# Weight splits moved behind the first graph's own steps, and more idle transposes on PE

## Chip, cores and metric

One core of a Trainium2 chip. The metric is the device time of the whole kernel in microseconds (us), median of several runs.

## What is computed

32 graphs of 256 nodes with 256 features go through four blocks, each with a residual and a layer norm. Cut to what matters here, for one graph (`x`, `adj`, all 256 x 256):

```
agg = adj @ x / deg(adj);   x1 = LN(x + relu([x, agg] @ W0^T))
h = relu(adj @ (x1 @ W1) + b1);  h = relu(adj @ (h @ W2) + b2)
x2 = LN(x1 + adj @ (h @ W3) + b3)
q, k, v = x2 @ W_qkv                      # 8 heads of 64
p = 0.33 * (softmax(q k^T / 8) + adj + exp(-adj))
x3 = LN(x2 + (p v) @ W_out + b_out)
q, k, v = x3 @ W3_qk^T, x3 @ W_v^T;  w = softmax(sum(q k^T * adj) / 8)
x4 = LN(x3 + w * v)
```

The graphs are independent of each other; the weights are shared.

## The kernel before

Matrix products run in fp32r with operands split in two: a high part (`_h`, a copy with rounding) and a low part (`_l`, the rest), and three products (hh, hl, lh) are summed. ACT makes every high part (`copy`, all recorded at L320), DVE every low part (`lo`, L555). PE's products are at L922 (`product`), 12 matmuls for one 256 x 256 x 256 product of nodes; they are called in two parts: HI (8 matmuls, needs only the high part of the operand that comes late) and LO (4 matmuls, needs the low part). Transposes of data are at L936, `keep_busy` is at L943: it transposes the identity into a bank that nobody reads, so many times.

Each engine has a hand-written list of steps, `slot(s)`, that runs for s = -2 to 35. Graph g's early steps stand in the lists of slot g - 1 and g, its attention and tail in slots g to g + 3, so that in the middle of the run each engine works on several graphs in turn. An engine executes its list strictly in order: a step that waits holds up all behind it. Only graph 0 runs nearly alone at the start. Its chain is: support0 (x @ W0's second half), sup0 split, aggregate (adj @ sup0), x1's norm (DVE, POOL, DVE), x1 transposes, then three layers of support (@ W1, W2, W3) and hidden / gcn_out (adj @ ...), x2's norm, x2 transposes, then the products with W_qkv.

The weights come by DMA and are split once, when g == 0. A count `act_w` tells how many high parts are done, `dve_w` how many low parts: w0 is 1; W1, W2, W3 are 2, 3, 4; the two halves of W_qkv (k = 0, 1) are 5, 6; W_out is 7; the last block's weight (w3) is 8. PE waits for these numbers in `weights(g, number)`. In the kernel before, the splits are attached to these steps of graph 0:

- ACT: w0 behind `x_hi`; W1, W2, W3 behind `sup0_hi`, and so ahead of `adj_hi`; both halves of W_qkv behind `x1_hi`; W_out and w3 behind `sup_hi(0)`.
- DVE: w0 behind `x_lo`; W1 behind `sup0_lo`, ahead of `adj_lo`; W2, W3 behind `norm_mean(0)`; W_qkv's halves behind `x1_lo` and `sup_lo(0)`; W_out and w3 behind `hidden_lo(0)`.

The order of ACT around it: x_hi(0), degrees(0), sup0_hi(0), adj_hi(0), adj_exp(0), self_copy(0), x1_hi(0), sup_hi(0), x_hi(1), hidden(0), hidden_hi(0), sup_hi(1), hidden(1), hidden_hi(1), sup_hi(2), x2_hi. That of DVE: x_lo(0), degrees(0), sup0_lo, adj_lo, aggregate, relu_residual, norm 0, x1_lo, sup_lo(0), adj_sum, hidden_lo(0), x_lo(1), sup_lo(1), x1_bias, hidden_lo(1), adj_extra, sup_lo(2), gcn_out, norm 1, x2_lo. `keep_busy` stands ahead of the mask columns (5), ahead of the loop (18), in front of the x1 transposes (40) and the x2 transposes (30) of graph 0, and in front of the last x3 transposes (30).

Of the kernel before, what the change touches and what calls it, by code (L numbers as in the profile page):

```python
# [13 lines left out]
def graph_blocks_kernel(nc, x, adj, nodemask, xT, adjT_in, L0_WT, L1_W1, L1_b1, L1_W2, L1_b2, L1_W3, L1_b3,  # L14
# [4 lines left out]
    FT = F // P  # L19
    D = 64  # L20
# [15 lines left out]
    with ctx:  # L36
        def sb(name, shape, dt=F32):
            return ctx.enter_context(nc.sbuf_tensor(name, shape, dt))
# [9 lines left out]
        w123_raw = sb("w123_raw", [P, 3, FT, F])  # L48
        work = sb("work", [P, 2, 2 * NT * 2 * N])
        wqkv_raw = work[:, :, 0:3 * INNER]  # L50
        wout_raw = sb("wout_raw", [P, PAIRS, F])
        w3_raw = sb("w3_raw", [P, FT, L3C])
# [11 lines left out]
        w123 = [sb(f"w123_{s}", [P, 3, FT, F], F32R) for s in "hl"]  # L64
        wqkv = [sb(f"wqkv_{s}", [P, FT, 3, INNER], F32R) for s in "hl"]
        wout = [sb(f"wout_{s}", [P, PAIRS, F], F32R) for s in "hl"]
        w3 = [sb(f"w3_{s}", [P, FT, L3C], F32R) for s in "hl"]
# [95 lines left out]
        def halves(ap):  # L163
            return ap.rearrange("p (a b) -> p a b", a=2)
# [37 lines left out]
        def once(g):  # L202
            return min(g + 1, G)
# [7 lines left out]
        def live(g):  # L211
            return 0 <= g < G

        def loaded(g):
            return 16 * (g // 2 + 1)

        def reuse(eng, semaphore, n):

            if n > 0:
                eng.wait_ge(semaphore, n)  # L220


        W0, W1, W2, W3TH, W_QKV, W_OUT, W_LAST = 1, 2, 3, 4, 5, 7, 8
# [94 lines left out]
        def _(act):  # L318
            def copy(dst, src, scale=1.0):
                return nc.scalar.activation(dst, src, ACT.Copy, scale=scale)  # L320

            def weight_hi(dst, src):
                return copy(dst, src).then_inc(act_w, 1)
# [18 lines left out]
            def adj_hi(g):  # L342
                if not live(g):
                    return
                act.wait_ge(dma_adjT[g % 2], loaded(g))
                reuse(act, pe_adjk, once(g - 2))
                copy(adjT[0][:, g % 2], adjT_sb[:, g % 2]).then_inc(act_adjT, 1)

            def degrees(g):
                if not live(g):  # L350
# [25 lines left out]
            def sup0_hi(g):  # L376
                if not live(g):
                    return
                act.wait_ge(pe_sup0, once(g))
                copy(sup[0][:, :, :], halves(bank(SUP0))).then_inc(act_sup0, 1)  # L380
                if g == 0:
                    act.wait_ge(dma_w123, 16 * 3)
                    for i in range(3):
                        weight_hi(w123[0][:, i], w123_raw[:, i])

            def self_copy(g):
                if not live(g):
# [4 lines left out]
            def x1_hi(g):  # L392
                if not live(g):
                    return
                act.wait_ge(pe_x1T, once(g))
                copy(fT[0][:, :, :], halves(bank(X1T))).then_inc(act_x1T, 1)
                if g == 0:
                    act.wait_ge(dma_wqkv, 16)
                    for k in range(FT):
                        weight_hi(wqkv[0][:, k].rearrange("p i (h d) -> p i h d", d=D),  # L400
                                  wqkv_raw[:, k].rearrange("p (h i d) -> p i h d", i=3, d=D))

            def sup_hi(layer, g):
                if not live(g):
                    return
                act.wait_ge(pe_sup[layer], once(g))
                copy(sup[0][:, :, :], halves(bank(SUP[layer]))).then_inc(act_sup[layer], 1)
                if g == 0 and layer == 0:
                    act.wait_ge(dma_wout, 16)
                    weight_hi(wout[0][:, :, :], wout_raw[:, :, :])  # L410
                    act.wait_ge(dma_w3, 16)
                    weight_hi(w3[0][:, :, :], w3_raw[:, :, :])
# [135 lines left out]
        def _(dve):  # L548
# [5 lines left out]
            def lo(dst, src, hi_part):  # L554
                return V_.tensor_tensor(dst, src, f32(hi_part), ALU.subtract)  # L555

            def weight_lo(dst, src, hi_part, number, last=True):
                dve.wait_ge(act_w, number)
                step = lo(dst, src, hi_part)
                if last:  # L560
                    step.then_inc(dve_w, 1)

            def wqkv_lo(k):
                for i in range(3):
                    weight_lo(wqkv[1][:, k, i].rearrange("p (h d) -> p h d", d=D),
                              wqkv_raw[:, k].rearrange("p (h i d) -> p i h d", i=3, d=D)[:, i],
                              wqkv[0][:, k, i].rearrange("p (h d) -> p h d", d=D), W_QKV + k, last=i == 2)
# [52 lines left out]
            def adj_lo(g):  # L620
                if not live(g):
                    return
                dve.wait_ge(act_adjT, once(g))
                reuse(dve, pe_adjk, once(g - 2))
                lo(adjT[1][:, g % 2], adjT_sb[:, g % 2], adjT[0][:, g % 2]).then_inc(dve_adjT, 1)

            def degrees(g):
                if not live(g):
# [25 lines left out]
            def sup0_lo(g):  # L654
                if not live(g):
                    return
                dve.wait_ge(act_sup0, once(g))
                lo(sup[1][:, :, :], halves(bank(SUP0)), sup[0][:, :, :]).then_inc(dve_sup0, 1)
                if g == 0:
                    weight_lo(w123[1][:, 0], w123_raw[:, 0], w123[0][:, 0], W1)  # L660

            def aggregate(g):
                if not live(g):
# [32 lines left out]
            def x1_lo(g):  # L696
                if not live(g):
                    return
                dve.wait_ge(act_x1T, once(g))
                lo(fT[1][:, :, :], halves(bank(X1T)), fT[0][:, :, :]).then_inc(dve_x1T, 1)  # L700
                if g == 0:
                    wqkv_lo(0)

            def sup_lo(layer, g):
                if not live(g):
                    return
                dve.wait_ge(act_sup[layer], once(g))
                lo(sup[1][:, :, :], halves(bank(SUP[layer])), sup[0][:, :, :]).then_inc(dve_sup[layer], 1)
                if g == 0 and layer == 0:
                    wqkv_lo(1)  # L710

            def hidden_lo(layer, g):
                if not live(g):
                    return
                dve.wait_ge(act_hid_hi[layer], once(g))
                lo(hidT[1][:, :, :], hid[:, :, :], hidT[0][:, :, :]).then_inc(dve_hid[layer], 1)
                if g == 0 and layer == 0:
                    weight_lo(wout[1][:, :, :], wout_raw[:, :, :], wout[0][:, :, :], W_OUT)
                    weight_lo(w3[1][:, :, :], w3_raw[:, :, :], w3[0][:, :, :], W_LAST)

            def gcn_out(g):
                if not live(g):
# [186 lines left out]
        def _(pe):  # L909
# [30 lines left out]
            def keep_busy(free_bank, count):  # L940

                for _ in range(count):
                    nc.tensor.transpose(bank(free_bank)[:, 0:P], ident[:, :], ident[:, :])  # L943
# [9 lines left out]
            def weights(g, number):  # L953
                if g == 0:
                    pe.wait_ge(dve_w, number)
# [41 lines left out]
            def x1_transpose(g):  # L997
                if not live(g):
                    return
                if g == 0:  # L1000
                    keep_busy(7, 40)
                pe.wait_ge(dve_x[0], once(g))
                transpose_tiles(bank(X1T), x1).then_inc(pe_x1T, 1)

            def support(layer, g, part):
                if not live(g):
                    return
                if part == HI:
                    weights(g, W1 + layer)
                    if layer == 0:  # L1010
                        pe.wait_ge(act_x1T, once(g))
                        reuse(pe, dve_scores, nth2(g - 1, 2, 1))
                    if layer == 1:
                        pe.wait_ge(act_hid_hi[0], once(g))
                    if layer == 2:
                        pe.wait_ge(act_hid_hi[1], once(g))
                else:
                    if layer == 0:
                        pe.wait_ge(dve_x1T, once(g))
                    if layer == 1:  # L1020
                        pe.wait_ge(dve_hid[0], once(g))
                    if layer == 2:
                        pe.wait_ge(dve_hid[1], once(g))
                last = nodes_product(bank(SUP[layer]), hidT if layer else fT, [w[:, layer] for w in w123], part)
                if part == LO:
                    last.then_inc(pe_sup[layer], 1)
# [228 lines left out]
            pe.wait_ge(pool_ident, 2)  # L1255
            keep_busy(7, 5)
            mask_columns()
            keep_busy(7, 18)
            for s in range(FIRST, LAST):
                slot(s)  # L1260

# [27 lines left out]
```

## Time and profile before

| | us |
|---|---|
| median of 3 runs | 1386.93 (1386.03 to 1387.05) |
| the profiled execution | 1388.81 |
| its span | 1387.0 |
| PE busy (matmuls) | 1358.5 (98%) |
| DVE busy | 1227.9 (89%) |
| ACT busy | 912.3 (66%) |
| POOL busy | 124.5 (9%) |

The span is from the first to the last instruction of one profiled execution. The profile has, for each engine, groups of instructions in order of time, the idle time ahead of a group and who ended it, and for stretches of time the busy time and PE's granted clock as a share of 2.4 GHz (0.50 is 1.2 GHz). PE is busy nearly throughout; the first 50 us and the last 50 us have gaps.

### The profile page before, as it was taken

How to read it: one execution, taken by the hardware profiler on the slowest of the kernel's cores; microseconds unless marked ns; L12 is line 12 of the kernel's file. 1: busy time of each engine (PE TensorE's matmuls, PEld its weight loads, DVE VectorE, ACT ScalarE, POOL GpSimd, SP SyncE). 2: the span in 40 equal slices, each digit the busy share in tenths (PEclk: the TensorE clock that was granted, in tenths of full speed). 3: DMA queues.
4: the chain of work that ended last, by engine and by line, in shares of the span. 5: the costliest groups of instructions: out<-in, count | busy, mean ns of one | idle time of the engine just before them, and what ended most of it. 6: DMA issues, size and time to landing. Idle time of an engine off the chain costs nothing.

```text
span 1387.0 us, 30079 instructions
## 1 busy us (share of the span) xinstructions
PE 1358.5 (98%) x11005; PEld 1196.8 (86%) x11005; DVE 1227.9 (89%) x3820; ACT 912.3 (66%) x2444; POOL 124.5 (9%) x265
## 2 busy tenths in 40 slices
PE   6999999999999999999999999999999999999996
PEld 6888889888889888889888889888889888889884
DVE  5689999999999999999999999999999999999985
ACT  4466776666776666776666777666776666776663
POOL 0000101101001101101101101101101101101101
PEclk9899999999999999999999999999999999999998
DMA  5111001111011111001111011111001111001000
GB/s 180 33 32 32 11 30 40 40 41 40 11 31 40 40 40 41 12 30 40 41 40 40 10 32 40 40 41 40 13 29 40 40 40 41 14 28 40 9 9 23
DMA packets 51313, 48.99 MB, mean 35 GB/s; under 512 B 7904, under 2 KB 50656, under 8 KB 51168
## 3 DMA queue, kind: packets, MB, share of 16 engines
q1 hardware_dynamic: 51168, 47.08, 10.7%
q8 instruction: 88, 1.44, 0.4%
q14 instruction: 57, 0.47, 0.1%
HBM read 38.68 MB, written 8.39 MB: 34 GB/s over the span
## 4 chain that ended last, share of the span: by engine, by line
PE 95%; ACT 2%; DVE 1%; issue 0%; DMA 0%; SPq 0%; POOL 0%; POOLq 0%; DVEq 0%
PE psum L922 63%; PE psum L936 12%; PE psum L1127 9%; PE psum L1104 8%; PE psum L1179 1%; PE psum L1182 1%; PE psum L1192 1%; PE psum L1201 0%; DMA w_raw<-in_L_gnn_W 0%; PE psum L943 0%; ACT work L454 0%; DVE work L767 0%; ACT wqkv_h L320 0%; ACT w_h L320 0%; DVE bn L571 0%
## 5 line engine op out<-in xcount | busy, mean ns | idle before, releaser
L454 ACT ACTIVATE work<-work,shift 128x256 f32<-128x256 f32 x512 | 253.9, 500 | 44.9 <-DVE shift L748 44.9
L767 DVE SCALAR_TENSOR_TENSOR work<-work,rsum,extra 128x256 f32<-128x256 f32 x512 | 221.2, 479 | 1.2
L748 DVE CUSTOM_DVE_ANT_0 work<-psum,minus_big 128x256 f32<-128x256 f32 x512 | 192.7, 419 | 16.5 <-PE psum L1104 15.4
L320 ACT ACTIVATE work<-psum 128x512 f32<-128x512 f32 x256 | 144.5, 594 | 9.7 <-PE psum L936 9.7
L922 PE MATMUL psum<-x2T_h,wqkv_h 128*128 128x256 f32 x512 | 148.7, 290 | 1.3 <-DVE x2T_l L555 1.2
L922 PE MATMUL psum<-x2T_l,wqkv_h 128*128 128x256 f32 x512 | 142.2, 278 | 0.0
L922 PE MATMUL psum<-x2T_h,wqkv_l 128*128 128x256 f32 x512 | 142.1, 278 | 0.0
L936 PE MATMUL psum<-ident,work 128*128 128x128 f32 x1024 | 139.7, 274 | 0.7 <-DVE work L767 0.7
L302 POOL TENSOR_TENSOR mv<-mv,eps 128x2 f32<-128x2 f32 x128 | 25.6, 200 | 1248.4 <-DVE mv L592 1248.4
L1127 PE MATMUL psum<-work,v_sb 128*64 128x256 f32 x1024 | 131.9, 389 | 0.9 <-ACT work L320 0.9
L320 ACT ACTIVATE sup_h<-psum 128x512 fp32r<-128x512 f32 x128 | 76.4, 597 | 74.0 <-PE psum L922 74.0
L555 DVE TENSOR_TENSOR sup_l<-psum,sup_h 128x512 fp32r<-128x512 f32 x128 | 88.1, 688 | 37.4 <-ACT sup_h L320 37.4
L936 PEld LDWEIGHTS psum<-ident,work 128*128 128x128 f32 x1024 | 113.5, 140 | 6.1 <-DVE work L767 1.3
L320 ACT ACTIVATE qkT_h<-psum 128x512 fp32r<-128x512 f32 x128 | 75.8, 592 | 39.0 <-PE psum L922 39.0
L922 PEld LDWEIGHTS psum<-x2T_h,wqkv_h 128*128 128x128 f32 x512 | 96.1, 188 | 6.1 <-DVE x2T_l L555 1.5
L922 PE MATMUL psum<-w_h,fT_h 128*128 128x256 f32 x384 | 100.1, 296 | 1.2 <-ACT fT_h L320 0.8
L305 POOL TENSOR_TENSOR rstd<-mv,minus_half 128x2 f32<-128x2 f32 x128 | 99.2, 775 | 10.0
L1127 PEld LDWEIGHTS psum<-work,v_sb 128*64 128x64 f32 x1024 | 64.9, 136 | 40.1 <-issue 6.9
L454 ACT ACTIVATION_READ_ACCUMULATOR work<-work,shift 128x1 f32 x512 | 97.8, 191 | 0.0
L571 DVE BATCH_NORM_STATS2 bn<-x_pre 128x6 f32<-128x256 f32 x256 | 95.8, 416 | 1.2
L922 PEld LDWEIGHTS psum<-x2T_l,wqkv_h 128*128 128x128 f32 x512 | 96.2, 188 | 0.0
L922 PEld LDWEIGHTS psum<-x2T_h,wqkv_l 128*128 128x128 f32 x512 | 96.1, 188 | 0.0
(130 smaller groups left out, 3806.2 us busy)
## 6 DMA issues: line engine op xcount, KB each, us to landing
xT_sb<-in_xT SPq DMA_DIRECT2D x32, 256.0 KB, 2.8
adjT_sb<-in_adjT SPq DMA_DIRECT2D x32, 256.0 KB, 3.1
adj_sb<-in_adj SPq DMA_DIRECT2D x32, 256.0 KB, 4.2
x_sb<-in_x SPq DMA_DIRECT2D x32, 256.0 KB, 4.4
out<-y_sb SPq DMA_DIRECT2D x32, 256.0 KB, 2.2
work<-in_L_gnn_W_qkv SPq DMA_DIRECT2D x1, 1536.0 KB, 9.8
mask_row<-in_nodemask SPq DMA_DIRECT2D x32, 32.0 KB, 4.1
w_raw<-in_L_gnn_W SPq DMA_DIRECT2D x3, 256.0 KB, 5.4
```

What stands on the lines that cost most here:

```text
L302: nc.gpsimd.tensor_tensor(mv[:, k, :, 1], mv[:, k, :, 1], eps[:, :], ALU.add) \
L305: nc.gpsimd.tensor_tensor(rstd[:, k], mv[:, k, :, 1], minus_half[:, :], ALU.pow) \
L320: return nc.scalar.activation(dst, src, ACT.Copy, scale=scale)
L454: last = nc.scalar.activation(prob[:, p % 2, i, h], prob[:, p % 2, i, h], ACT.Exp, bias=shift[:, p % 2, h, i:i + 1], scale=-1.0, accum_out ...
L555: return V_.tensor_tensor(dst, src, f32(hi_part), ALU.subtract)
L571: last = V_.bn_stats(out=bn[:, k, t], in_=src[:, t])
L748: last = V_.tensor_tensor_reduce(out=prob[:, p % 2, i, h], in0=bank(SCORES[p] + h)[:, i * N:(i + 1) * N], in1=minus_big[:, g % 2, i], scal ...
L767: last = V_.scalar_tensor_tensor(out=prob[:, p % 2, i, h], in0=prob[:, p % 2, i, h], scalar=rsum[:, p % 2, h, i:i + 1], in1=extra[:, g % 2 ...
L922: last = mm(dst, left, right, start=opens and n == 0, stop=closes and n == len(steps) - 1)
L936: last = nc.tensor.transpose(dst[:, r * N + t * P:r * N + (t + 1) * P], src[:, t, block_of(r)], ident[:, :])
L1104: last = mm(bank(SCORES[p] + h)[:, i * N:(i + 1) * N], qkT[left][rows, p % 2, 0, block_of(i)], qkT[right][rows, p % 2, 1], start=n == 0 an ...
L1127: last = mm(bank(PV[p])[h * D:(h + 1) * D, 0:N], v_sb[:, k, (2 * p + h) * D:(2 * p + h + 1) * D], probT[:, p % 2, h, k], start=k == 0, sto ...
```

## The change

All edits are for graph 0 or ahead of the loop:

- ACT: W1, W2, W3 are copied behind `adj_hi` instead of `sup0_hi`; the W_qkv halves one by one behind `sup_hi(0)` and `sup_hi(1)` instead of both behind `x1_hi`; W_out and w3 behind `sup_hi(2)` instead of `sup_hi(0)`.
- DVE: W1's low part behind `adj_lo` instead of `sup0_lo`; the W_qkv halves behind `sup_lo(0)` and `sup_lo(1)` instead of `x1_lo` and `sup_lo(0)`; W_out and w3 behind `sup_lo(2)` instead of `hidden_lo(0)`.
- PE: `keep_busy` 40 to 44 in front of the x1 transposes; 12 new ones in front of support 1 and of support 2, each; 18 to 21 ahead of the loop.

No transfer, semaphore or count is changed. The functions `degrees` to `sup0_hi` of ACT, which the printed diff moves, are the same text.

```diff
             def adj_hi(g):
                 copy(adjT[0][:, g % 2], adjT_sb[:, g % 2]).then_inc(act_adjT, 1)
+                if g == 0:
+                    act.wait_ge(dma_w123, 16 * 3)
+                    for i in range(3):
+                        weight_hi(w123[0][:, i], w123_raw[:, i])
...
             def sup0_hi(g):
                 copy(sup[0][:, :, :], halves(bank(SUP0))).then_inc(act_sup0, 1)
-                if g == 0:
-                    act.wait_ge(dma_w123, 16 * 3)
-                    for i in range(3):
-                        weight_hi(w123[0][:, i], w123_raw[:, i])
...
             def x1_hi(g):
-                if g == 0:
-                    act.wait_ge(dma_wqkv, 16)
-                    for k in range(FT):
-                        weight_hi(wqkv[0][:, k].rearrange("p i (h d) -> p i h d", d=D),
-                                  wqkv_raw[:, k].rearrange("p (h i d) -> p i h d", i=3, d=D))
...
             def sup_hi(layer, g):
-                if g == 0 and layer == 0:
+                if g == 0 and layer < 2:
+                    act.wait_ge(dma_wqkv, 16)
+                    weight_hi(wqkv[0][:, layer].rearrange("p i (h d) -> p i h d", d=D),
+                              wqkv_raw[:, layer].rearrange("p (h i d) -> p i h d", i=3, d=D))
+                if g == 0 and layer == 2:
                     act.wait_ge(dma_wout, 16)
                     weight_hi(wout[0][:, :, :], wout_raw[:, :, :])
                     act.wait_ge(dma_w3, 16)
...
             def adj_lo(g):
+                if g == 0:
+                    weight_lo(w123[1][:, 0], w123_raw[:, 0], w123[0][:, 0], W1)
...
             def sup0_lo(g):
-                if g == 0:
-                    weight_lo(w123[1][:, 0], w123_raw[:, 0], w123[0][:, 0], W1)
...
             def x1_lo(g):
-                if g == 0:
-                    wqkv_lo(0)
...
             def sup_lo(layer, g):
-                if g == 0 and layer == 0:
-                    wqkv_lo(1)
+                if g == 0 and layer < 2:
+                    wqkv_lo(layer)
+                if g == 0 and layer == 2:
+                    weight_lo(wout[1][:, :, :], wout_raw[:, :, :], wout[0][:, :, :], W_OUT)
+                    weight_lo(w3[1][:, :, :], w3_raw[:, :, :], w3[0][:, :, :], W_LAST)
...
             def hidden_lo(layer, g):
-                if g == 0 and layer == 0:
-                    weight_lo(wout[1][:, :, :], wout_raw[:, :, :], wout[0][:, :, :], W_OUT)
-                    weight_lo(w3[1][:, :, :], w3_raw[:, :, :], w3[0][:, :, :], W_LAST)
...
             def x1_transpose(g):
                 if g == 0:
-                    keep_busy(7, 40)
+                    keep_busy(7, 44)
...
             def support(layer, g, part):
                 if part == HI:
+                    if g == 0 and layer:
+                        keep_busy(7, 12)
                     weights(g, W1 + layer)
...
             keep_busy(7, 5)
             mask_columns()
-            keep_busy(7, 18)
+            keep_busy(7, 21)
```

## Rows read from the trace of the kernel before

**Rows 1.** The page: the span.

```profile
span 1387.0 us, 30079 instructions
```

**Rows 2.** Windows, stretch, length, busy PE, PEld, DVE, ACT, POOL, clock, DMA.

```profile
60.00:1340.00 1280.00, 1278.55 (x10445) 1127.19 (x10444) 1164.98 (x3637) 864.93 (x2330) 117.46 (x244) 1.00 0.10 32
```

**Rows 3.** Timeline of ACT: start, us, what, [idle before <-releaser]; around adjT.

```profile
11.20 1.67 ACT L320 ACTIVATE w_h<-w_raw 128x512 fp32r<-128x512 f32 x3 [1.04 <-DMA w_raw<-in_L_gnn_W]
12.77 0.61 ACT L320 ACTIVATE adjT_h<-adjT_sb 128x512 fp32r<-128x512 f32 x1
...
13.81 0.57 ACT L320 ACTIVATE self_part<-psum 128x512 f32<-128x512 f32 x1
```

**Rows 4.** Timeline of ACT, from x1's transposes to the first hidden layer.

```profile
23.33 2.85 ACT L320 ACTIVATE wqkv_h<-work 128x1536 fp32r<-128x1536 f32 x2
...
26.55 1.06 ACT L320 ACTIVATE wout_h<-wout_raw 128x1024 fp32r<-128x1024 f32 x1
...
28.75 0.84 ACT L421 ACTIVATE hid<-psum,b_col 128x256 f32<-128x256 f32 x2
29.62 0.63 ACT L320 ACTIVATE hidT_h<-hid 128x512 fp32r<-128x512 f32 x1
```

**Rows 5.** Timeline of DVE, first graph.

```profile
10.19 0.69 DVE L555 TENSOR_TENSOR sup_l<-psum,sup_h 128x512 fp32r<-128x512 f32 x1 [1.66 <-ACT sup_h L320]
...
16.81 0.88 DVE L668 SCALAR_TENSOR_TENSOR x_pre<-psum,rdeg,self_part 128x256 f32<-128x256 f32 x2 [2.70 <-PE psum L922]
...
24.84 1.90 DVE L555 TENSOR_TENSOR wqkv_l<-work,wqkv_h 128x512 fp32r<-128x512 f32 x3 [0.69 <-ACT wqkv_h L320]
...
30.89 1.22 DVE L555 TENSOR_TENSOR wout_l<-wout_raw,wout_h 128x1024 fp32r<-128x1024 f32 x1
32.03 0.95 DVE L555 TENSOR_TENSOR w_l<-w_raw,w_h 128x768 fp32r<-128x768 f32 x1
...
43.99 0.69 DVE L725 TENSOR_TENSOR x_pre<-psum,x_b 128x512 f32<-128x512 f32 x1 [2.29 <-PE psum L922]
...
46.84 0.74 DVE L608 TENSOR_SCALAR x<-x_pre,mv,rstd 128x256 f32<-128x256 f32 x2 [1.08 <-POOL rstd L305]
```

**Rows 6.** Timeline of PE, first graph: first row of each burst, transposes.

```profile
14.21 0.35 PE L922 MATMUL psum<-sup_h,adjT_h 128*128 128x256 f32 x1 [3.28 <-ACT adjT_h L320]
...
16.48 5.34 PE L943 MATMUL psum<-ident 128*128 128x128 f32 x40
22.14 0.66 PE L936 MATMUL psum<-ident,x 128*128 128x128 f32 x4 [0.31 <-DVE x L608]
...
26.72 0.39 PE L922 MATMUL psum<-adjT_h,sup_h 128*128 128x256 f32 x1 [1.53 <-ACT sup_h L320]
...
30.40 0.36 PE L922 MATMUL psum<-w_h,hidT_h 128*128 128x256 f32 x1 [1.98 <-ACT hidT_h L320]
...
32.84 0.58 PE L922 MATMUL psum<-adjT_h,sup_h 128*128 128x256 f32 x1 [0.69 <-ACT sup_h L320]
...
37.44 0.55 PE L922 MATMUL psum<-w_h,hidT_h 128*128 128x256 f32 x1 [1.68 <-ACT hidT_h L320]
...
47.86 0.60 PE L936 MATMUL psum<-ident,x 128*128 128x128 f32 x4
...
49.97 0.36 PE L922 MATMUL psum<-x2T_h,wqkv_h 128*128 128x256 f32 x1
```

**Rows 7.** Windows, PE alone: stretch, length, busy (matmuls), granted clock, DMA.

```profile
1.60:7.40 5.80, 5.76 (x25) 1.00 0.87 277
14.80:18.00 3.20, 3.20 (x18) 0.50 0.90 356
18.20:21.80 3.60, 3.60 (x33) 1.00 0.92 342
25.20:31.60 6.40, 2.90 (x22) 1.00 0.00 0
31.80:45.40 13.60, 10.54 (x47) 0.50 0.00 0
```

## The prediction

> **What bounds the kernel now.** I read the page first, for the span [rows 1], then the busy time of each engine in one long stretch, then the beginning engine by engine. From 60 to 1340 us PE is busy 1278.55 of 1280 us [rows 2]. DVE has 1164.98 and ACT 864.93 in the same stretch. The reader is to see that all 32 graphs after the start are one gapless queue on PE: the time is the moment at which PE becomes gapless, plus a fixed queue, plus a tail. The change leaves queue and tail as they are (every edited line stands under `g == 0` or ahead of the loop), so an earlier start of the gapless stretch is worth its whole length, and an earlier ACT or DVE alone is worth nothing. That stretch begins with the first query and key product at 49.97 [rows 6]. I follow that product back.
>
> PE's rows of the first graph show short bursts, each waiting for ACT: 3.28 us before the aggregation, then 1.53, 1.98, 0.69 and 1.68 us [rows 6]. The bursts cost by the granted clock. The one from 30.40 takes 1.75 us (32.84 less its 0.69 idle), the one from 32.84 takes 2.92 (37.44 less 1.68), for the same 12 matmuls. The clock is at 2.4 GHz (1.00) from 18.2 and at 1.2 GHz (0.50) from 31.8 to 45.4 [rows 7]. So the change can gain in two ways: shorter waits, and bursts at the higher level.
>
> **Part 1, adj_hi ahead of the three W1..W3 copies.** Before, ACT waits for the DMA of the last of them until 11.20, spends 1.67 us on three copies, and only then copies adjT (12.77); DVE's adj_lo follows and PE's aggregation starts at 14.21 [rows 3, 6]. After, adj_hi stands behind sup0_hi. DVE's sup_l starts at 10.19 [rows 5], so sup_h is finished by then and ACT starts adjT_h there: done at about 10.8, the lo part of 0.69 us at 11.5, PE at about 11.6. The burst costs 1.7 us if the clock holds (2.3 at the old level), so it ends at 13.3. The three copies still start at 11.20, as their DMA sets them. What was 12.77 (adjT_h, 0.61) isn't between them and self_part any more, so self_part moves from 13.81 to 13.29 and ends at 13.86 [rows 3]. DVE's aggregate step needs both; it is self_part now that comes last, and the step starts at 13.93 instead of 16.81 [rows 5]: **2.88 us**. W1's lo part, moved behind adj_lo, runs before that in DVE's wait and costs nothing. Three more idle transposes ahead of the loop cost 3 x 0.23 = 0.7 us (25 took 5.8, [rows 7]). If none of it lies in PE's wait for w0, the burst ends at 14.0, 0.1 past self_part; if all of it does, nothing is late. I take nothing.
>
> **Part 2, wqkv's halves out of x1_hi and x1_lo.** From DVE's aggregate step to the end of support 0 nothing else changes: the x1 transposes come 5.33 us after the step (22.14 - 16.81), at 19.26, and support 0 ends 3.05 us behind them (25.19, which is 26.72 less 1.53, minus 22.14) [rows 5, 6], at 22.31. Then ACT's sup_hi was held up by the two wqkv copies, 2.85 us from 23.33 [rows 4]; the wait of PE was 1.53, where the undisturbed one of the next layer is 0.69. After, it is 0.68, so hidden 0 starts at 22.99: another **0.85 us**, 3.73 in sum against 26.72. It takes 1.70 (28.42 - 26.72) and ends at 24.69. One wqkv copy (half of 2.85, with x_hi of 0.5 behind it) now lies between: 22.9 to 24.8, so hidden's ReLU starts at 24.8 instead of 24.72, nearly free. ReLU and hidT_h take 0.84 and 0.63 [rows 4]; support 1 starts at 26.39. Before 30.40: **4.0 us**.
>
> **Part 3, the clock from there.** DVE does wqkv_lo(0) from 24.36 (1.90 us, [rows 5]), then adj_sum (0.6), so hidden_lo starts at 26.8, some 0.5 late; support 1's last four matmuls wait until 27.55, and it ends at 28.25, 0.1 later than without. The first half of wqkv being enough for none of PE's work, nobody else waits. hidden 1: 28.25 + 0.69 = 28.93, ends 30.63 at the higher level. ACT has wqkv(1) from 28.8 to 30.2, inside that burst: free. ReLU and copy, 1.67 with gaps (37.44 - 35.76): support 2 starts at 32.30. DVE: wqkv_lo(1) to 32.1, x1_bias to 32.7, hidden_lo until 33.4, so the last part of support 2 starts at 33.5 and it ends at 34.15, 0.1 to 0.3 late. gcn_out starts at 34.83 and ends at 36.53. Before, gcn_out's sum in DVE started at 43.99 [rows 5].
>
> **Part 4, what is late next: wout and w3.** They now stand behind sup_lo(2), in front of DVE's gcn_out step. ACT copies wout 34.7 to 35.75 (1.06, [rows 4]), DVE's lo parts follow at 35.82 for 1.22 and 0.95 (0.08 less back to back) [rows 5] and end at 37.83. The gcn_out step is ready at 36.55 and so waits **1.3 us** behind them, and all that hangs on it: bn, POOL, x2, x2T. Step at 37.83 instead of 43.99: 6.16 earlier. From it to x2 ready takes 3.59 (46.84 + 0.74 - 43.99, [rows 5]): 41.42. Before, PE's 30 idle transposes still stood in front of x2's own, by 0.2 us (47.86 against 47.63, [rows 6]). After they end near 39.5, and x2's start at 41.47; the first query product follows 2.11 behind (49.97 - 47.86), with support 0 of the next graph in between as before: 43.6. That is **49.97 - 43.6 = 6.4 us** less.
>
> **The transposes in the waits** (12 and 12 new, 40 made 44) are 0.11 us each at 2.4 GHz (33 in 3.6 us) and up to 0.23 at 1.2 [rows 7]: 12 are 1.3 us in waits of 1.7, free; at 1.2 GHz they would be 2.6 to 2.8 and outlast the wait by about 1.0. The 44 run from 13.3 to 18.2, and leave 1.0 us idle before 19.26.
>
> The Trainium skill, "TensorE: Matmul & The Clock Gate", Part 4, states that transpose mode doesn't count as PE being busy for the gate. By that rule these transposes would be useless or worse, and the time (c)'s, below. The trace speaks against it: the clock was at 0.50 from 14.8 to 18.0, the transposes began at 16.48, and at 18.2 to 21.8, with 33 of them and nothing else on PE, it was 1.00 [rows 6, 7].
>
> Does the gain add up to the end? The loads of graph 2 are released by the first graph's steps and shift with them. The profiled execution took 1388.81 us for a span of 1387.0, 1.9 above the median of the runs, 1386.93. I take the difference of spans from the median: 1386.93 - 6.35 = 1380.6.
>
> **Rivals.**
> (a) The clock falls once. Before, it fell after 25.2 to 31.6, where PE was busy 2.90 of 6.40 us [rows 7]. The forecast has two thin stretches: 18.2 to 23.0 (idle 1.0, 0.8, 0.7 between short bursts) and 39.5 to 42 (idle 1.9). Neither is quite like the stretch that lost the clock, and neither is as full as those that kept it; the trace doesn't settle it. If it falls near 21.5, hidden 0 costs 2.92 for 1.70 (1.2) and 12 transposes outlast their wait (up to 1.6 more, less once the clock is back; PE is then busy without a gap): 1.2 to 2.8, I take 2.0. If it falls at 42, PE is busy from there, and before, it was low in such a busy stretch for at least the 3.2 us from 14.8 to 18.0 [rows 7], at half speed: 1.6 to 1.7 lost. So 1382.3 to 1382.6 us.
> (b) It falls in both: 1380.6 + 3.7 = 1384.3.
> (c) Slower than before: idle transposes don't hold the clock, and at the low level they are in the way. Decides if PE stays at 0.50 from the x1 wait on. Then hidden 0, support 1, hidden 1, support 2 and gcn_out cost 1.2 more each (6.0), support 0's rest 0.5, the two twelves 1.0 each, less 1.3 since wout's parts are hidden again: gcn_out's sum at 37.83 + 7.2 = 45.0, and the 30 transposes behind it at 0.23 (6.9) end at 51.8 against 47.9 before, so +3.9: 1390.8. Its condition is what the page states; the windows of 14.8 to 21.8 [rows 7] speak against it.
> (d) The splits don't hold DVE or ACT up as I say: wout and w3 cost gcn_out nothing: 1.3 us more gain, 1379.3. Or the first stretch is set by other DMAs than now, and only the clock and 0.85 us are gained: some 3.5, 1383.4.
>
> **How the numbers follow.** Forecast 1380.6: chance 0.43. (a) 0.32, (b) 0.12, (c) 0.04, (d) 0.04 for its first, 0.05 for its second. Range 1379.4 to 1384.4: it leaves out (c), (d)'s first and up to half of (b), 0.14 in all. The forecast's own range is 1380.0 to 1381.4. 0.2% of this kernel, 2.8 us, is about what a measurement can tell: faster means below 1384.2. Forecast, (a), (d) and half of (b) lie there: 0.43 + 0.32 + 0.09 + 0.06 = 0.90; within 0.2% the rest of (b), 0.06; slower (c), 0.04.
>
> **What would show it.** DVE's aggregate step at 13.9 with self_part just before it (part 1). PE's wait before hidden 0 at 0.7 (part 2). Granted clock 1.00 from 18 to 40, and bursts of 1.7 us (part 3). wout_l and w_l right in front of gcn_out's sum, PE long done (part 4). First query product at 43.6, then the same gapless queue. A clock of 0.50 anywhere between 20 and 46 is (a) or (b). The prediction is wrong if PE's gapless stretch begins 6 us earlier and the end doesn't move with it.

## The result and the profile after

| | before | changed |
|---|---|---|
| median of 10 runs | 1386.80 us (1384.73 to 1387.54) | 1383.65 us (1382.49 to 1384.66) |
| ratio, changed to before | | 0.9977, 95% interval 0.9968 to 0.9986 |
| the profiled execution | 1388.81, span 1387.0 | 1384.66, span 1382.9 |

The change gains 3.15 us by the medians and 4.1 us from one profiled span to the other. The measured 1383.65 us lies within the range, and the direction is right. But the forecast was 1380.6 us, and half of the gain it named (6.2) isn't there in the median.

The middle is what it was. PE's window of the changed kernel (stretch, length, busy, granted clock, DMA):

```profile
60.00:1340.00 1280.00, 1278.52 (x10444) 1.00 0.10 32
```

The first query product, the row of PE's timeline that answers to the last of [rows 6]:

```profile
45.90 0.36 PE L919 MATMUL psum<-x2T_h,wqkv_h 128*128 128x256 f32 x1
```

PE is as gapless as in [rows 2], and the gapless stretch begins at 45.90 instead of 49.97: 4.07 us earlier, for a span 4.1 us shorter. From that product to the end both profiles take 1337.0 us, so all of the gain comes from the first 46 us. (One gap of 0.43 to 0.44 us, 4.5 us behind the product, is in both.) ACT's timeline in the changed kernel, which answers to [rows 3]:

```profile
9.80 0.63 ACT L320 ACTIVATE adjT_h<-adjT_sb 128x512 fp32r<-128x512 f32 x1
11.51 1.68 ACT L320 ACTIVATE w_h<-w_raw 128x512 fp32r<-128x512 f32 x3 [1.08 <-DMA w_raw<-in_L_gnn_W]
...
13.61 0.57 ACT L320 ACTIVATE self_part<-psum 128x512 f32<-128x512 f32 x1
```

DVE's, which answers to [rows 5]:

```profile
14.21 0.88 DVE L667 SCALAR_TENSOR_TENSOR x_pre<-psum,rdeg,self_part 128x256 f32<-128x256 f32 x2 [1.35 <-ACT self_part L320]
...
38.10 1.22 DVE L554 TENSOR_TENSOR wout_l<-wout_raw,wout_h 128x1024 fp32r<-128x1024 f32 x1 [0.26 <-ACT wout_h L320]
39.24 0.95 DVE L554 TENSOR_TENSOR w_l<-w_raw,w_h 128x768 fp32r<-128x768 f32 x1
40.11 0.68 DVE L722 TENSOR_TENSOR x_pre<-psum,x_b 128x512 f32<-128x512 f32 x1
```

adjT is copied ahead of the three weights, and DVE's aggregate step starts at 14.21 instead of 16.81, now released by self_part. The low parts of W_out and w3 stand without a gap in front of gcn_out's sum at 40.11 (43.99 before). Timeline of PE, which answers to [rows 6]:

```profile
12.83 4.97 PE L940 MATMUL psum<-ident 128*128 128x128 f32 x44
19.54 0.66 PE L933 MATMUL psum<-ident,x 128*128 128x128 f32 x4 [1.74 <-DVE x L607]
...
24.26 0.58 PE L919 MATMUL psum<-adjT_h,sup_h 128*128 128x256 f32 x1 [0.69 <-ACT sup_h L320]
...
26.98 2.05 PE L940 MATMUL psum<-ident 128*128 128x128 f32 x12
...
38.71 3.44 PE L940 MATMUL psum<-ident 128*128 128x128 f32 x30
43.74 0.66 PE L933 MATMUL psum<-ident,x 128*128 128x128 f32 x4 [1.59 <-DVE x L607]
```

PE's windows in the same kernel, in the columns of [rows 7]:

```profile
12.80:17.80 5.00, 5.00 (x46) 1.00 1.05 387
17.80:21.00 3.20, 0.69 (x5) 1.00 1.03 375
21.50:28.00 6.50, 5.81 (x27) 0.50 0.05 18
28.50:50.00 21.50, 17.98 (x147) 1.00 0.14 40
```

After 5 us without a gap PE has 0.69 us of work in 3.20, and then the clock is at 0.50, from before 21.5 until past 28.0. Most of support 0 (from 20.97) and all of hidden 0 (from 24.26) run in that stretch at 1.2 GHz. That is rival (a) in its first form.

### The profile page after: what moved, and what is told of

It reads as the page before. It is cut to its first block, busy times and chain, and to the rows that moved or that the text cites. A ratio compares the mean times of both kernels' runs of the same rounds, so it can differ in the third digit from the quotient of the medians.

```text
span 1382.9 us, 30141 instructions
## 1 busy us (share of the span) xinstructions
PE 1358.4 (98%) x11036; PEld 1197.1 (87%) x11036; DVE 1227.9 (89%) x3820; ACT 912.5 (66%) x2444; POOL 124.4 (9%) x265
## 4 chain that ended last, share of the span: by engine, by line
PE 95%; DVE 2%; ACT 1%; DMA 0%; issue 0%; SPq 0%; POOL 0%; POOLq 0%; DVEq 0%
PE psum L919 63%; PE psum L933 12%; PE psum L1126 9%; PE psum L1103 8%; PE psum L1178 1%; PE psum L1181 1%; PE psum L1191 1%; PE psum L1200 0%; DMA w_raw<-in_L_gnn_W 0%; ACT work L453 0%; DVE work L764 0%; DVE bn L570 0%; POOL rstd L305 0%; DVE x L607 0%; DVE wqkv_l L554 0%
```

## The experiments

Each kernel is the changed one with the edit shown, unless it says otherwise. The runs come from three sets, each on one chip and with the kernel before beside it. The row "changed" without a set is the result above, whose kernel before had 1386.80 us. Medians of different sets aren't strictly comparable: the time from the first query product to the end is 1336.9 to 1337.3 us in the ten profiles of before, the result and the first two sets, and 1338.1 to 1338.2 in the four of the third. No edit reaches there, and the changed kernel itself has 1337.0 in the result and 1338.1 in the third set, so times of the third set are some 1.2 us longer for that alone. "The twelves" are the 12 idle transposes in front of support 1 and of support 2. The ratios to before are those on record with the runs and aren't exactly the quotients of the medians.

Each run also gives its mean granted clock over the span. It is the number to group by, since it says how long an execution was at 1.2 GHz: 0.001 is 2.8 us of it. Part of that is the tail, where PE has little left to do.

```
kernel                        set  median   range               mean granted clock of the runs
before                        1    1387.28  1385.87 to 1391.18  0.988 to 0.995
before                        2    1387.03  1384.03 to 1391.53  0.986 to 0.996
before                        3    1387.71  1386.52 to 1392.37  0.990 to 0.996
changed                       -    1383.65  1382.49 to 1384.66  0.994 x4, 0.995 x2, 0.996 x4
x1 wait 58                    1    1383.24  1382.42 to 1384.51  0.996 x2, 0.997 x3
moves only                    1    1386.16  1382.19 to 1388.96  0.988 to 0.997
transposes only               1    1386.66  1385.49 to 1387.30  0.994 x7, 0.995 x1, 0.996 x3
low parts late                1    1381.45  1380.85 to 1382.90  0.996 x2, 0.997 x3
x1 wait 0                     2    1385.56  1383.62 to 1386.14  0.991 x2, 0.992 x7, 0.994 x2
part 1 undone                 2    1385.36  1383.95 to 1386.79  0.994 x4, 0.995 x4, 0.996 x3, 0.997 x1
part 2 undone                 2    1384.06  1383.09 to 1385.63  0.994 x3, 0.995 x1, 0.996 x6, 0.997 x1
part 1 alone                  2    1383.95  1382.62 to 1385.46  0.993 to 0.997
changed again                 3    1385.58  1383.62 to 1386.65  0.994 x1, 0.995 x4, 0.996 x3, 0.997 x3
58, no twelves                3    1383.85  1383.39 to 1386.97  0.992 x2, 0.995 x1, 0.996 x2, 0.997 x6
58 and low parts late         3    1382.78  1382.40 to 1383.41  0.997 x5
the same, W_qkv's lo later    3    1383.43  1382.88 to 1384.54  0.996 x1, 0.997 x4
```

**58 idle transposes in the x1 wait.** Does the idle stretch ahead of 21 us lose the clock?

```diff
-                    keep_busy(7, 44)
+                    keep_busy(7, 58)
```

> The changed kernel with 58 idle transposes instead of 44 in PE's wait for x1. Theory (the clock falls near 21 us because PE sits idle for 1.7 us there): 14 more at 0.11 us fill 1.5 of the 1.7 us, PE's granted clock stays at 1.00 from 8 us to the tail in every run, the first query product starts near 44.0 instead of 45.9, median 1382.5 against 1383.65 and no run above 1383. Rival (idle transposes don't count for the clock, or the 3.15 us gained are all there is): still 0.50 from 21 to 28, median 1383.7.

Measured 1383.24, ratio to before 0.9963 (0.9949 to 0.9977). PE's windows in its profile:

```profile
13.00:19.60 6.60, 6.60 (x63) 1.00 0.98 354
20.00:50.00 30.00, 24.20 (x198) 1.00 0.21 63
```

The start of x2's transposes in its timeline:

```profile
41.55 0.66 PE L933 MATMUL psum<-ident,x 128*128 128x128 f32 x4 [1.58 <-DVE x L607]
```

The mechanism is as expected: the clock at 1.00 from 13 us to the tail, no run below 0.996 where the changed kernel has six of ten, x2's transposes at 41.55 instead of 43.74, and a span of 1380.6. The median moved by 0.4 us and not by the 1.2 I expected. The two medians come from different sets (against its own set's before this kernel gains 4.04 us, the changed one 3.15), and three of the five runs are above 1383 (one at 1384.51), which I had ruled out. The 58 also outlast the wait a little: x1's transposes start 5.46 us behind DVE's aggregate step here and 5.33 in the changed kernel.

**No idle transposes in the x1 wait.**

```diff
-                    keep_busy(7, 44)
+                    keep_busy(7, 0)
```

> The changed kernel with no idle transposes in PE's wait for x1 (44 to 0), so that PE is idle there for some 6.6 us. Theory (idle transposes hold the clock): PE's granted clock falls to 0.50 in this wait in every run, and comes back only at the 12 transposes or later: 3 to 7 us more at the low level than the changed kernel's quickest runs, quickest run 1384 or above (1382.5 with 44), median 1385 to 1386. Rival (transposes don't count as work for the clock): the same as with 44, quickest 1382.5, median 1383.7.

Measured 1385.56, ratio 0.9988 (0.9979 to 0.9997); the quickest run is 1383.62, where I had 1384 or above, and every run is at 0.994 or below. PE's timeline at x1's transposes:

```profile
19.90 1.12 PE L933 MATMUL psum<-ident,x 128*128 128x128 f32 x4 [6.55 <-DVE x L607]
```

Its windows:

```profile
16.00:28.80 12.80, 7.43 (x32) 0.50 0.47 175
30.00:50.00 20.00, 16.53 (x131) 1.00 0.10 27
```

Idle for 6.55 us, PE is at 1.2 GHz from 16.0 to 28.8. The same wait filled with 58 transposes and nothing else keeps 2.4 GHz (13.0 to 19.6, above). Idle transposes do hold the clock here, and that is worth about 2 us of median (1.9 against the 44 and 2.3 against the 58, which are from other sets). By the Trainium skill, "TensorE: Matmul & The Clock Gate", Part 4, transpose mode doesn't count as PE being busy: by that, the two kernels would behave alike. The measurement decides against it for these fp32 transposes.

**The moves without the new transposes.** The splits as moved; 18, 40 and no twelves, as before.

```diff
-                    if g == 0 and layer:
-                        keep_busy(7, 12)
...
-                    keep_busy(7, 44)
+                    keep_busy(7, 40)
...
-            keep_busy(7, 21)
+            keep_busy(7, 18)
```

> The moved splits alone; idle transposes as before (18 ahead of the loop, 40 before x1, none before support 1 and 2). Theory (shorter waits give 4 us only if the clock holds, and the transposes hold it): the clock falls near 21 and stays at 0.50 until gcn_out or later, since nothing fills the waits of the hidden layers; five bursts at 2.9 instead of 1.7 us: 1382.5 + 6 - 1.3 = about 1387, no gain over before. Rival (the moves are the gain, the transposes are decoration): 1383.5 to 1384.

Measured 1386.16, ratio 0.9984 (0.9972 to 0.9997). Neither theory had this: the runs lie 6.8 us apart, in the order of their clock almost without exception. Two at 0.997 took 1382.19 and 1382.65, as quick as the changed kernel ever is; the two at 0.990 and 0.988 took 1388.66 and 1388.96. The profiled one is of the quick kind. A window of PE, and the start of x2's transposes:

```profile
20.00:50.00 30.00, 21.57 (x174) 1.00 0.21 65
```

```profile
41.60 0.66 PE L933 MATMUL psum<-ident,x 128*128 128x128 f32 x4 [1.59 <-DVE x L607]
```

The clock held though PE idles 1.97 us in front of x1's transposes and 1.75 and 1.68 us where the twelve are missing. So the same program on the same chip keeps the clock or loses it, from one execution to the next. What the moves shorten doesn't need the transposes, but having it in the median does.

**The transposes without the moves.** The kernel before, with 21, 44, 12 and 12.

```diff
-                    keep_busy(7, 40)
+                    keep_busy(7, 44)
...
+                    if g == 0 and layer:
+                        keep_busy(7, 12)
```

> The kernel before with the new idle transposes alone (21, 44, 12, 12), splits where they were. Theory: the clock that before loses from 31.8 to 45.4 us holds or comes back early, four bursts at 1.7 instead of 2.9 us: 3 to 5 us gained, median 1382 to 1384, all of it from the clock. Rival (the moves are the gain): 1386.8.

Measured 1386.66, ratio 0.999 (0.9982 to 0.9999). My theory missed: 0.6 us and not 3 to 5. PE's windows in its profile:

```profile
8.00:13.50 5.50, 2.78 (x24) 1.00 0.83 265
14.00:20.50 6.50, 5.36 (x25) 0.50 1.02 373
21.00:50.00 29.00, 23.43 (x189) 1.00 0.05 12
```

The start of the aggregation in its timeline:

```profile
15.14 0.55 PE L922 MATMUL psum<-sup_h,adjT_h 128*128 128x256 f32 x1 [4.36 <-ACT adjT_h L320]
```

The hidden layers do keep the clock now (21 to 50 at 1.00), which the profile of before didn't. The stretch in front of the aggregation, 4.36 us idle, still loses it, and the waits are as long as ever. Two things explain the small gain: the profiled execution of before, from which I took the 3 to 5 us, had lost more of the clock than most do, and the transposes can't save what part 1 saves.

**Low parts of W_out and w3 late.**

```diff
-                if g == 0 and layer == 2:
-                    weight_lo(wout[1][:, :, :], wout_raw[:, :, :], wout[0][:, :, :], W_OUT)
-                    weight_lo(w3[1][:, :, :], w3_raw[:, :, :], w3[0][:, :, :], W_LAST)
...
             def x2_lo(g):
+                if g == 0:
+                    weight_lo(wout[1][:, :, :], wout_raw[:, :, :], wout[0][:, :, :], W_OUT)
                 dve.wait_ge(act_x2T, once(g))
                 lo(x2T[1][:, :, :], halves(bank(X2T)), x2T[0][:, :, :]).then_inc(dve_x2T, 1)
+                if g == 0:
+                    weight_lo(w3[1][:, :, :], w3_raw[:, :, :], w3[0][:, :, :], W_LAST)
```

> The changed kernel with the low part of W_out in front of x2_lo and that of w3 behind it, instead of both in front of DVE's gcn_out. Theory (gcn_out's sum waits 1.4 us for them and is on the path): the sum starts when PE ends, near 38.8 instead of 40.1, PE's wait behind the 30 transposes falls from 1.6 to 0.2 us, and the median is 1.3 lower, 1382.3. Rival (hidden under the 30 idle transposes of PE, which end at 42.1): 1383.65.

Measured 1381.45, ratio 0.9952 (0.9936 to 0.9967): the quickest kernel of the study against its own runs of before. DVE's timeline in its profile:

```profile
36.62 0.69 DVE L719 TENSOR_TENSOR x_pre<-psum,x_b 128x512 f32<-128x512 f32 x1 [1.07 <-PE psum L920]
...
40.11 1.22 DVE L554 TENSOR_TENSOR wout_l<-wout_raw,wout_h 128x1024 fp32r<-128x1024 f32 x1
41.58 0.69 DVE L554 TENSOR_TENSOR x2T_l<-psum,x2T_h 128x512 fp32r<-128x512 f32 x1 [0.25 <-ACT x2T_h L320]
```

PE's:

```profile
40.25 0.66 PE L934 MATMUL psum<-ident,x 128*128 128x128 f32 x4 [0.40 <-DVE x L607]
```

The sum starts with PE's end, at 36.62. In the profile of the kernel with 58, whose clock is equally held, it starts at 37.92, and x2's transposes at 41.55 against 40.25: 1.30 us in both. Of these, 0.10 were there before: gcn_out's product starts at 34.98 with 58 and at 34.88 here. The wait itself is worth 1.2 us, and PE's idle time behind the 30 transposes falls by as much, from 1.59 to 0.40. The low part of W_out now ends 0.25 us before x2T_l is wanted. The median is 2.2 us below the changed kernel's (1.8 below that with 58, on the same chip), more than the 1.3 I expected. Part of the 2.2 is that none of these five runs is below 0.996, with the same 44 transposes in front of x1, which this edit doesn't touch; the rest isn't explained.

**Part 1 undone.** The three copies and W1's low part back behind sup0_hi and sup0_lo.

```diff
                 copy(adjT[0][:, g % 2], adjT_sb[:, g % 2]).then_inc(act_adjT, 1)
-                if g == 0:
-                    act.wait_ge(dma_w123, 16 * 3)
...
                 copy(sup[0][:, :, :], halves(bank(SUP0))).then_inc(act_sup0, 1)
+                if g == 0:
+                    act.wait_ge(dma_w123, 16 * 3)
```

> The changed kernel with part 1 undone: W1, W2, W3 split behind sup0_hi and sup0_lo again, ahead of adj_hi and adj_lo. Theory (part 1 is worth 2.6 to 2.9 us of waits, and is the bulk): DVE's aggregate step back near 16.8 instead of 14.2, quickest run 1385.2 against 1382.5; with the clock lost ahead of the aggregation as before, median 1386.3 or above. Rival (the gain is mostly the clock's, and the wait is refilled later): within 1 us of the changed kernel, 1384 to 1384.5.

Measured 1385.36, ratio 0.999 (0.9982 to 0.9999). The aggregate step in DVE's timeline:

```profile
18.24 0.88 DVE L667 SCALAR_TENSOR_TENSOR x_pre<-psum,rdeg,self_part 128x256 f32<-128x256 f32 x2 [3.13 <-PE psum L919]
```

It is past the 16.8 of before, since the weights' DMA landed late in this execution too and the clock was lost ahead of the aggregation. Against its own set's before, this kernel gains 1.67 us and the changed one 3.15, so part 1 carries about half of the gain. I had expected less to be left: a median above 1386.3 and a quickest run of 1385.2, which was 1383.95. By the runs at 0.996 (1385.17 here, 1382.88 in the changed kernel) part 1 is worth 2.3 us, by the medians 1.5 to 1.7. The profiles show where the rest of its 2.9 us goes. Here the clock is lost ahead of the aggregation (0.50 from 14 to 20 us) and is back for the hidden layers: from the copies of W1 to W3 to the aggregate step it takes 6.04 us (5.61 in before, 2.70 in the changed kernel), and from that step to x2's transposes 27.67. The changed kernel loses the clock behind the step and needs 29.53 for the same way, 27.59 with 58.

**Part 2 undone.** Both W_qkv halves back behind x1_hi, in DVE behind x1_lo and sup_lo(0).

```diff
                 copy(fT[0][:, :, :], halves(bank(X1T))).then_inc(act_x1T, 1)
+                if g == 0:
+                    act.wait_ge(dma_wqkv, 16)
+                    for k in range(FT):
...
-                if g == 0 and layer < 2:
-                    wqkv_lo(layer)
+                if g == 0 and layer == 0:
+                    wqkv_lo(1)
```

> The changed kernel with part 2 undone: both halves of W_qkv split behind x1_hi, and in DVE behind x1_lo and sup_lo(0), again. Theory: PE's wait before hidden 0 back at 1.5 us instead of 0.7 (0.85 more), of which 0.3 to 0.4 comes back since DVE has no W_qkv step ahead of x1_bias and hidden_lo(1): 0.4 to 0.8 slower by the quickest runs, median 1384.2. Rival (nothing waited for it in the end): 1383.65.

Measured 1384.06, ratio 0.9976 (0.9966 to 0.9987). PE's timeline before hidden 0, and before x2's transposes:

```profile
24.39 0.39 PE L922 MATMUL psum<-adjT_h,sup_h 128*128 128x256 f32 x1 [1.80 <-ACT sup_h L320]
...
42.43 0.66 PE L936 MATMUL psum<-ident,x 128*128 128x128 f32 x4 [1.59 <-DVE x L608]
```

From x1's transposes (19.55) to these of x2 it takes 22.88 us; with 58 and part 2 in, 22.13 (41.55 - 19.42), both with the clock held. Part 2 is worth 0.75 us on the path, of which ACT's wait for the DMA of W_qkv in this execution is 0.16. The medians put it at 0.4, and the gains against each one's own before at 0.2, both inside their uncertainty.

**Part 1 alone, with the new transposes.** Both halves of W_qkv as above, W_out and w3 back behind sup_hi(0) and hidden_lo(0). (What the expectation calls part 3 is part 4 of the prediction.)

```diff
-                if g == 0 and layer == 2:
+                if g == 0 and layer == 0:
                     act.wait_ge(dma_wout, 16)
```

> Parts 2 and 3 undone: only the W1 to W3 splits moved, and all the new idle transposes. Theory (part 3 moved 1.3 us of wait in front of gcn_out's sum, which eats what part 2 gained): W_out and w3 split early again, gcn_out's sum starts when PE ends; 0.85 lost before hidden 0 and 1.3 to 1.4 gained before x2: by the quickest runs 0.3 to 0.6 faster than the changed kernel, 1382.0, median 1383.2. Rival (parts 2 and 3 are a gain): 1384.3 to 1385.

Measured 1383.95, ratio 0.9982 (0.9974 to 0.9991). Neither side: not the 0.3 to 0.6 us quicker of my theory (quickest 1382.62, expected 1382.0), nor the rival's 1384.3. Two rows of its timeline say why, the first of ACT:

```profile
21.80 2.86 ACT L320 ACTIVATE wqkv_h<-work 128x1536 fp32r<-128x1536 f32 x2 [1.25 <-DMA work<-in_L_gnn_W_qkv]
```

and one of DVE:

```profile
40.22 0.69 DVE L725 TENSOR_TENSOR x_pre<-psum,x_b 128x512 f32<-128x512 f32 x1 [1.06 <-PE psum L922]
```

The second is as I had it: gcn_out's sum no longer waits for low parts. The first is new. With part 1 in, ACT is at W_qkv nearly 3 us sooner than before, ahead of its DMA, and waits 1.25 us for it. The copy of x1's support stands behind, and PE waits for it before hidden 0:

```profile
25.20 0.58 PE L922 MATMUL psum<-adjT_h,sup_h 128*128 128x256 f32 x1 [2.12 <-ACT sup_h L320]
```

In the kernel before, that DMA had landed 2.2 us before ACT came to it (issued at 11.3, 9.8 us to landing, copies from 23.33). So part 2 also takes a DMA wait off the path that part 1 had uncovered, 0.16 us in the profile with only part 2 undone and 1.25 here.

**The changed kernel again**, beside the next three.

> The changed kernel itself, beside the three others of this set on one chip. Expected median 1383.3 to 1384.0, quickest run near 1382.5, runs with 0 to 7 us of low clock at the start.

Measured 1385.58 (ratio 0.9978, 0.9969 to 0.9987), above the median I had expected. The recorded ratio is the one first measured, but by the medians the gain is 2.13 us here and was 3.15. The interval of each ratio reaches 1.2 us to either side, so the two gains don't contradict each other, and neither is known to better than about a microsecond. One row of ACT in its profile:

```profile
12.21 1.67 ACT L320 ACTIVATE w_h<-w_raw 128x512 fp32r<-128x512 f32 x3 [1.08 <-DMA w_raw<-in_L_gnn_W]
```

The last of W1 to W3 was there at 12.2; the other profiles have 11.20 to 12.20. self_part, and with it x1, follow it one to one (DVE's aggregate step at 14.92 here, 2.71 behind the copies; at 13.96 with 58, where they start at 11.25). It is the second thing that differs between executions, beside the clock, which this one lost too (x1's transposes at 20.24 behind an idle 1.72 us, the clock at 0.50 from 22.7 to 29.1).

**58, but no twelves.**

```diff
-                    if g == 0 and layer:
-                        keep_busy(7, 12)
...
-                    keep_busy(7, 44)
+                    keep_busy(7, 58)
```

> 58 idle transposes before x1, none before support 1 and 2. Theory (each wait needs its own filling, since the clock is decided again and again): some runs lose the clock in the hidden layers, where each loses 3 us or more for want of a gapless stretch: quickest 1382.4, median 1384 to 1385.5, slowest above 1387. Rival (the x1 wait alone decides, the two twelves are idle decoration): all runs 1382.4 to 1384, as with 58 and both twelves.

Measured 1383.85, ratio 0.9973 (0.9964 to 0.9982). Nine of the eleven runs are at 0.995 or above, within 1.3 us of each other; two lost the clock, at 1386.2 and 1387.0. The profiled one is one of them; PE's windows:

```profile
20.00:28.00 8.00, 4.74 (x34) 1.00 0.25 86
29.00:42.00 13.00, 9.95 (x44) 0.50 0.00 1
43.00:50.00 7.00, 6.91 (x59) 1.00 0.24 77
```

This is the stretch of 0.50 that the profile of before shows [rows 7]: once lost among the hidden layers' bursts it stays lost for 13 us, until the idle transposes before x2. The twelves are an insurance, rarely needed once x1's wait is full. The theory's mechanism holds; its median (1384 and more) was too high and its quickest run (1382.4, measured 1383.39) too low.

**58 and the low parts late.** The edits of the first and fifth experiment together.

> 58 idle transposes before x1, and W_out's and w3's low parts behind gcn_out's sum. Theory (two independent terms: clock 0.4 to 1.0 by the median, wait 1.3): median 1381.1, spread under 2 us, faster than each alone (1383.24 and 1381.45). Rival (not additive, since with the shorter x2 wait the clock is safe anyway): 1381.45.

Measured 1382.78, ratio 0.9963 (0.9951 to 0.9976). Beside the changed kernel on the same chip it is 2.80 us quicker. If the wait is worth its 1.2, 1.6 are left for the clock; the split is a subtraction and not measured by itself. All five runs have 0.997, and they lie 1.0 us apart. The absolute 1381.1 missed by 1.7, of which this chip's longer rest explains 1.2, and whether it beats the late low parts with 44 isn't shown: the intervals of their ratios, from two chips, overlap.

**W_qkv's low parts behind hidden_lo.**

```diff
-                if g == 0 and layer < 2:
-                    wqkv_lo(layer)
...
                 lo(hidT[1][:, :, :], hid[:, :, :], hidT[0][:, :, :]).then_inc(dve_hid[layer], 1)
+                if g == 0:
+                    wqkv_lo(layer)
```

> As the one before, and W_qkv's low parts behind hidden_lo(0) and hidden_lo(1) instead of sup_lo(0) and sup_lo(1), so that DVE has hidden's low part in time. Theory (DVE is late by 0.1 to 0.3 us for support 1 and support 2): 0.2 to 0.4 faster than the one before, unless sup_lo(1) and sup_lo(2) now come late by as much. Rival: the delay only moves to sup_lo: no difference.

Measured 1383.43, ratio 0.9968 (0.9956 to 0.9981): not quicker than the one before, as the rival said. PE's timeline shows that it waits for the other low part now:

```profile
36.35 0.74 PE L920 MATMUL psum<-sup_l,adjT_h 128*128 128x256 f32 x4 [0.30 <-DVE sup_l L554]
```

Behind sup_lo, DVE's 1.9 us make hidden's low part up to some 0.1 us late; behind hidden_lo, they make sup's 0.3 late in two layers. From x1's transposes to the first query product the profile has 23.64 us, and 23.18 in the one before.

## Why the prediction was right and where it was wrong

**The bound.** Right. The start of PE's gapless stretch and the span moved together: 4.07 and 4.1 us for the changed kernel, 6.26 (43.71 for the first query product) and 6.4 for the kernel with 58.

**Part 1, 2.88 us.** Right in its order: self_part comes last, and 1.35 us of DVE's wait end with it. The step moved 2.60 in the profile shown, and 2.85 in the profile with 58; the difference is the DMA of the weights, which let the copies start at 11.51 and 11.25 instead of 11.20. Counted from these copies the step comes 2.70 behind instead of 5.61. As a worth in the median it was too high: 1.5 to 2.3 us, since where the clock is lost moves with it (see "Part 1 undone").

**Part 2, 0.85 us.** The wait is 0.69 where I had 0.68. The DMA of W_qkv, which would have come on the path next, wasn't in my working.

**Part 4, 1.3 us late for gcn_out.** Right, and 0.1 too high: 1.2 by the experiment that takes it away.

**Part 3, the clock held.** This step failed, for six of the ten runs, the profiled one among them. With the clock held, the forecast's times are met: x2's transposes at 41.47 forecast and 41.55 measured with 58, the first query product at 43.6 and 43.71, span 6.35 less forecast and 6.4 less measured. With the clock lost, it is rival (a): near 21 us as I had it, and x2's transposes come 2.19 us later than with 58 (43.74 against 41.55), of which 0.25 are the later weights, while 0.13 are missing since the 58 outlast their wait: 2.1 for the clock. I had 2.0, in part by luck. Hidden 0 does cost 1.2 more (2.72 us against 1.53), but the rest was to be the 12 transposes outlasting their wait, and they didn't: support 1 follows hidT_h as closely as with 58. It is support 0, which takes 2.60 us instead of 1.63.

One term had the thin stretch too full: PE was to idle 1.0 us ahead of x1's transposes and idled 1.74. The aggregation started at 11.33 and took 1.5 us, where I had 11.6 and 1.7, so that the 44 ended at 17.80 and not at 18.2, and x1's transposes came 0.28 later. The length of that wait alone doesn't decide, though: the profiles with 1.97 us (moves alone) and 1.69 (part 2 undone) kept the clock, those with 1.74, 1.72 (the changed kernel, twice) and 1.38 (part 1 alone) lost it. What was wrong was to think that one execution decides it: the kernel with the moves alone shows executions of both kinds. What decides between them stays open.

The 0.23 us for a transpose "at 1.2 GHz" is from a row of [rows 7] whose clock reads 1.00, the 25 at the start of the kernel. It entered only the rivals. In the changed kernel the first 12 took 2.05 us, with the clock back about half way.

**The reference.** The other step that failed: "I take the difference of spans from the median." The profiled execution of before took 1388.81, 2.0 above the median of ten. I wrote it off as an offset. It was an execution that had lost more clock than most, 0.990 over its span. In the set of 22 runs of before, those at 0.993 to 0.995 took 1385.9 to 1388.3, those at 0.988 to 0.991 took 1388.9 to 1391.2. So a difference of two profiles, 6.4, held some 2 us that the median of before never had to lose. Taken from the profiled execution, the same 6.35 give 1382.46, and the changed kernel's four runs at 0.996 took 1382.49 to 1383.16. 3.15 is made of about 3.9 (from 1386.80 to the median of these four, 1382.88) less about 0.8 that its own lost clocks take back from the median. That the measured 1383.65 lies in the range is owed to the room left for (a) and (b), since the reference wasn't among the things in doubt.

**The other rivals.** (c) is ruled out by the two kernels with 0 and 58 transposes. (b) was not seen in a profile: in none of them is the clock lost between the 30 transposes and x2. (d)'s first form is what moving the low parts of W_out and w3 gives, not what the change does; its second, 1383.4, nearly names the measured time by a mechanism that didn't happen.

## What to carry to other kernels

Where a start-up chain runs alone on the chip, look which weight is prepared ahead of which step: an in-order engine should do what the chain needs first and prepare weights in the waits that follow, and the last one not in front of the chain's next step (1.2 us here). Where the clock of TensorE is lost behind an idle stretch of 1 to 2 us, fill the stretch to its end: with 58 transposes of 0.11 us and the twelves, all 15 runs of three kernels are at 0.996 or above; with 44, 11 of the changed kernel's 21 are at 0.995 or below. And before a difference is taken from one profile, hold its time against the other runs of the same kernel; 2 us apart means another execution than the usual one.

## What the runs showed of the hardware

The same program loses or keeps the 2.4 GHz clock from one execution to the next: 1382.19 to 1388.96 us for the moves alone, at mean granted clocks of 0.997 to 0.988. The size of it was unexpected, 6.8 us in a kernel whose median moved by 3.

Where it comes back differs too. In the profile with 58 and no twelves the clock stayed at 0.50 for 13 us among bursts with waits of 0.7 and 1.7 us between them, though PE was busy for 9.95 of 13.00. In the changed kernel, where 12 transposes fill the second of these waits, it was back in under 7 us (5.81 busy of 6.50).

And the same weights' DMA lets ACT start its copies of W1 to W3 at 11.20 to 12.21 us in the profiles (11.51 and 12.21 in the two of the changed kernel), which moves the whole chain with it.
